# Causal mask products of two self attentions: weights of 32 rows by 128 columns instead of 32 by 32

## What is computed

```python
scores = jnp.einsum('bhqd,bhkd->bhqk', q, k) / math.sqrt(hd)
causal = jnp.tril(jnp.ones((l, l), bool))
scores = jnp.where(causal, scores, -jnp.inf)
att = jax.nn.softmax(scores, axis=-1)
out = jnp.einsum('bhqk,bhkd->bhqd', att, v)
```

## Time and profile before

| | |
|---|---|
| median of 3 runs | 839.37 us (839.31 to 840.55) |
| the profiled execution | 838.6 us |
| its span, first to last instruction | 836.8 us |
| mean granted TensorE clock | 0.998 |
| PE busy | 807.1 us (96%) |
| DVE, ACT, POOL busy | 537.8, 400.9, 261.3 us |
| mask products (line 967) | 1024 matmuls, 19.8 us busy |

### The profile page before, as it was taken

One profiled execution on the slowest core, in us unless ns is written; L12 is line 12 of the kernel. 1 busy time (PEld: TensorE's weight loads), 2 busy tenths in 40 slices (PEclk: granted clock), 3 DMA queues, 4 the chain that ended last, 5 costly groups with the idle time before them and its releaser, 6 DMA issues.

```text
span 836.8 us, 23981 instructions
## 1 busy us (share of the span) xinstructions
PE 807.1 (96%) x10073; PEld 662.7 (79%) x10073; DVE 537.8 (64%) x1379; ACT 400.9 (48%) x989; POOL 261.3 (31%) x311
## 2 busy tenths in 40 slices
PE   8999999999999999999998998999999999999995
PEld 6888887675547787777777787989998899989983
DVE  6675666587886676677776744574466546654666
ACT  4554444558773344455555334463454245424542
POOL 0221422569976632112222368640000100010001
PEclk9999999999999999999999999999999999999999
DMA  9310002222220200000000112330000010000001
GB/s 314 139 53 16 16 22 68 83 52 76 74 63 26 76 20 7 22 22 18 19 18 29 31 40 80 100 102 27 2 3 2 2 52 2 2 1 28 2 2 50
DMA packets 21002, 36.85 MB, mean 44 GB/s; under 512 B 3200, under 2 KB 7424, under 8 KB 20640
## 3 DMA queue, kind: packets, MB, share of 16 engines
q1 hardware_dynamic: 20800, 35.20, 13.6%
q10 hardware_dynamic: 96, 0.13, 0.1%
HBM read 30.86 MB, written 2.10 MB: 39 GB/s over the span
## 4 chain that ended last, share of the span: by engine, by line
PE 81%; DVE 7%; ACT 4%; issue 2%; POOL 2%; DMA 1%; SPq 1%; ACTq 0%; POOLq 0%; DVEq 0%
PE bank L840 16%; PE bank L842 15%; PE bank L841 15%; PE bank L997 6%; PE bank L1277 5%; PE bank L1247 4%; PE bank L1261 3%; PE bank L1017 3%; PE bank L1134 2%; PE bank L1002 2%; DVE tank L2342 1%; PE bank L967 1%; PE bank L1121 1%; PE bank L1298 1%; PE bank L859 1%
## 5 line engine op out<-in xcount | busy, mean ns | idle before, releaser
L840 PE MATMUL bank<-wr,hTl 128*128 128x512 f32 (+3 forms) x392 | 153.3, 391 | 1.3 <-issue 0.8
L842 PE MATMUL bank<-wr,hTh 128*128 128x512 f32 (+3 forms) x392 | 146.9, 375 | 0.0
L841 PE MATMUL bank<-wr,hTh 128*128 128x512 f32 (+3 forms) x392 | 146.5, 374 | 0.0
L1584 ACT ACTIVATE pT<-bank 128x512 f32<-128x512 f32 x128 | 70.0, 604 | 95.1 <-PE bank L967 95.0
L2342 DVE TENSOR_REDUCE tank<-bank 128x4 f32<-128x512 f32 x128 | 82.1, 683 | 42.4 <-PE bank L967 42.4
L840 PEld LDWEIGHTS bank<-wr,hTl 128*128 128x128 f32 (+1 forms) x392 | 73.6, 188 | 17.9 <-issue 5.3
L842 PEld LDWEIGHTS bank<-wr,hTh 128*128 128x128 f32 (+1 forms) x392 | 73.7, 188 | 12.5
L840 PE MATMUL bank<-hTh,wr 128*128 128x256 f32 (+1 forms) x272 | 83.1, 306 | 0.0
L841 PEld LDWEIGHTS bank<-wr,hTh 128*128 128x128 f32 (+1 forms) x392 | 73.8, 188 | 11.2 <-issue 1.0
L841 PE MATMUL bank<-hTl,wr 128*128 128x256 f32 (+1 forms) x272 | 81.0, 298 | 0.0
L842 PE MATMUL bank<-hTh,wr 128*128 128x256 f32 (+1 forms) x272 | 81.0, 298 | 0.0
(11 more groups left out here) (250 smaller groups left out, 1763.8 us busy)
## 6 DMA issues: line engine op xcount, KB each, us to landing
raw<-w_qkv_dram SPq DMA_DIRECT2D x12, 256.0 KB, 2.9
raw<-w_xq_dram SPq DMA_DIRECT2D x16, 192.0 KB, 2.4
raw<-w_xo_dram SPq DMA_DIRECT2D x12, 256.0 KB, 2.8
cin<-xT_dram SPq DMA_DIRECT2D x8, 256.0 KB, 3.9
x_all<-x_dram SPq DMA_DIRECT2D x8, 256.0 KB, 6.6
cin<-ctx_dram SPq DMA_DIRECT2D x8, 256.0 KB, 3.4
cin<-ctxT_dram SPq DMA_DIRECT2D x8, 256.0 KB, 3.3
out_dram<-x_all SPq DMA_DIRECT2D x8, 256.0 KB, 2.1
```

The lines of the kernel that those rows point to most:

```text
L840: mm(dst, lhs[1], rhs[0], start=start, stop=False)
L841: mm(dst, lhs[0], rhs[1], start=False, stop=False)
L842: return mm(dst, lhs[0], rhs[0], start=False, stop=stop)
L1584: av(pT[e][:, 2 * rows + n, :], t_bank[n][:, :], ACT.Exp).then_inc(exp_ready, 1)
```

## The change

The masks' weights are now slices of a banded matrix `band16` (128 partitions by 224 columns, bf16): 96 columns of zeros, the 32 by 32 identity once in each group of partitions, 96 columns of zeros. The slice of 128 columns that begins at column `96 - 32 * g` has the identity in its columns `32 * g` to `32 * g + 31` and zeros elsewhere. A mask product now writes all 128 partitions at the columns of block `g`: what it adds is the triangle in the block's partitions and zero in the others. Its weights have 32 rows and 128 columns, as a score product's, and it takes the same row group as the scores of its bank. The number of mask products stays (16 in a paired step, 8 in an unpaired one) and so do their moving columns (128). They are issued block by block, the straight and the turned ones of one block together; `scores_psum` and `shifted_psum` are incremented after the last block.

The identity blocks come in 32 more columns of the array `masks`; POOL sets the zeros with two memsets in its first microsecond or so, DVE casts 32 columns where it cast 128, and PE waits for these four instead of two. `band16` takes 192 bytes more per partition than `ident16`; what is allocated after it moves by as much.

```diff
-    masks = np.concatenate([np.eye(P), later, sooner], 1)
+    masks = np.concatenate([np.eye(P), later, sooner, np.tile(np.eye(PAD), (GROUPS, 1))], 1)
...
-        ident16, causal16 = sb("ident16", [P, P], BF16), sb("causal16", [P, 2, PAD], BF16)
+        BAND = P - PAD
+        band16, causal16 = sb("band16", [P, BAND + P], BF16), sb("causal16", [P, 2, PAD], BF16)
...
-        causal = view(1, 3840, 2 * PAD)
+        causal = view(1, 3840, 3 * PAD)
...
-        TABLES, EARLY, ROWS = 2, 3, 3
+        TABLES, EARLY, ROWS = 4, 3, 3
...
-            def hide_later(banks, turned_over):
+            def hide_later(banks, turned_over, rows, g, stop):
+
+                at = slice(g * PAD, (g + 1) * PAD)
                 for n in range(2):
-                    for g in range(GROUPS):
-                        rows = (g + 2 * turned_over + n) % GROUPS
-                        at, of = slice(g * PAD, (g + 1) * PAD), slice(rows * PAD, (rows + 1) * PAD)
-                        ins = mm(tiles(banks[n][:, :])[at, :, at], ident16[of, of],
-                                 causal16[of, turned_over, :].unsqueeze(1).broadcast_to([PAD, KT, PAD]), start=False, stop=True,
-                                 skip_group_check=True)
+                    of = slice((2 * rows + n) * PAD, (2 * rows + n + 1) * PAD)
+                    ins = mm(tiles(banks[n][:, :])[:, :, at], band16[of, BAND - g * PAD:BAND - g * PAD + P],
+                             causal16[of, turned_over, :].unsqueeze(1).broadcast_to([PAD, KT, PAD]), start=False, stop=stop,
+                             skip_group_check=True)
                 return ins
...
-                if scored(i):
-                    hide_later(s_bank, 0).then_inc(scores_psum, 1)
-                if scored(j):
-                    hide_later(t_bank, 1).then_inc(shifted_psum, 1)
+                for g in range(GROUPS):
+                    last = g == GROUPS - 1
+                    if scored(i):
+                        ins = hide_later(s_bank, 0, rows, g, True)
+                        if last:
+                            ins.then_inc(scores_psum, 1)
+                    if scored(j):
+                        ins = hide_later(t_bank, 1, rows_c, g, True)
+                        if last:
+                            ins.then_inc(shifted_psum, 1)
...
+            nc.gpsimd.memset(band16[:, 0:BAND], 0.0).then_inc(tables_ready, 1)
+            nc.gpsimd.memset(band16[:, BAND + PAD:], 0.0).then_inc(tables_ready, 1)
...
-                v.tensor_copy(ident16[:, :], ident[:, :]).then_inc(tables_ready, 1)
-                v.tensor_copy(causal16[:, :, :], causal.rearrange("p (a t) -> p a t", a=2)).then_inc(tables_ready, 1)
+                v.tensor_copy(band16[:, BAND:BAND + PAD], causal[:, 2 * PAD:]).then_inc(tables_ready, 1)
+                v.tensor_copy(causal16[:, :, :], causal[:, 0:2 * PAD].rearrange("p (a t) -> p a t", a=2)).then_inc(tables_ready, 1)
```

## The result

The changed kernel is slower: 844.17 us median (843.94 to 844.82, 4 runs) against 839.34 us (838.84 to 840.55, 4 runs), a ratio of 1.0055 with a 95% interval of 1.0042 to 1.0068, so +4.6 us (3.5 to 5.7). The prediction was 841.9 us, in a range of 840.2 to 854.4, with 0.72 on slower. The direction and the range held; the loss is nearly twice the forecast 2.5 us. The question for the experiments is where the other part came from.

A forecast was written before the change was run, and what follows sets the result against it. PE's own stream, busy 96% of the span, was taken as the bound. Entry saved against four rounds gave 54 × 0.027 + 20 × 0.05 = +2.5 us on the median 839.37, so 841.9 us, range 840.2 to 854.4.

The forecast's parts named there:

- PE's stream is the path in both self attentions: Both self attentions: a nanosecond between last score product and first product behind the masks goes into the end nearly whole.
- rival E: Mask places: if DVE or ACT set the steps' length, the time stays; chance held within 0.15 for same.
- 54 paired, 20 unpaired places: Both self attentions: 1024 mask products make 54 paired places of 16 products and 20 unpaired ones of 8.
- Entry saved, exit kept: Around the masks: tile shape change on entering (0.11 us) goes; the one on leaving stays, 0.155 us to the next work.
- Rival C: Entering the masks: fp32 to bf16 stops the array as a new shape does; 8.1 us more, +10.6 us; chance 0.05.
- Pace of a round 0.056 us: Masks' four rounds over four row groups: 128 columns' streaming sets 0.056 us a round, if weight loads keep up.
- A: Mask rounds: weight loads set the pace, 0.112 us a round; in all +14.9 us, 854.3; chance 0.15.
- B: Mask rounds: the load hides only in part, 0.084 us a round; +8.7 us, 848.1; chance 0.07.
- D: Mask rounds: they overlap, so entry is saved and nothing paid; −8 us, 831.4; chance 0.13.
- The sum, +0.027 and +0.05 us a place, +2.5 us: Mask places: 54 paired at +0.027 us and 20 unpaired at +0.05 us, 1.5 + 1.0 = +2.5 us.
- The rest at nothing, ±0.3 us: Outside the mask rounds: later releases of maxima and exponentials, POOL's memsets, DVE's cast, a larger DMA; nothing, ±0.3 us.
- its 0.15 for "same": Whole kernel: chance 0.15 that the time lies within 1.7 us of before; faster 0.13, slower 0.72.

The follow-up runs named there:

- the two kernels with the old pace of the projections: Changed kernel with band16 allocated last, all other tiles at their old places: +0.6 us; changed kernel with 64 bytes more, 256 in all: +1.3 us; both against the kernel before.

## Why the prediction was right or wrong

- *PE's stream is the path in both self attentions.* Right for 76% of added time (13.8 of 18.1 us) and 60 to 67% of removed time (8.4 to 9.3 of 13.9 us), not "nearly whole". The step that was too strong took a few us of waits as negligible; they are small in sum, but they grow and shrink by 4 us with a stream that is 14 to 18 us shorter or longer. For the masks' 1.9 us, +0.6 and +1.3 us were measured in the two kernels with the old pace of the projections, so rival E holds for a part of the places.
- *54 paired, 20 unpaired places.* Right, read from the count.
- *Entry saved, exit kept.* Right: 0.12 us in place of 0.22, and 0.144 us out. Rival C is out. The Trainium skill, "TensorEngine Tiling (Array Packing)", section Tiling Modes, says that a change of mode drains the engine and a change of tile alone does not. The trace agrees: the delay on entering went with the change of mode, and the one on leaving stayed with it.
- *Pace of a round 0.056 us.* Right: by the start times a row group's products come 55 to 56 ns apart, and with it A, B and D fall. The Trainium skill, "TensorE: Matmul & The Clock Gate", section Back-to-back issue gap, gives about 81 ns a product for a stream of pairs of load and matmul with 128 columns. That figure doesn't carry over to rounds over four row groups here: 56 ns a round, with its four loads.
- *The sum, +0.027 and +0.05 us a place, +2.5 us.* Measured are 0.019 and 0.045 us, +1.9 us. The term that was mis-sized is the exit, 0.144 for 0.155, 0.8 us over 74 places; why it is shorter from tiles of 32 by 128 than from 32 by 32 is not shown. (The paired place was also rounded up: 430.875 less 430.85 is 0.025, not 0.027, 0.1 us in the sum.)
- *The rest at nothing, ±0.3 us.* This is the step that failed. It listed waits, memsets, a cast and a DMA, and of the allocation it said nothing, though the description of the change has it: all that is allocated after `band16` moves by 192 bytes. That is +4.9 us in the projections' start sum, +4.7 us (3.5 to 6.0) of time by itself, and nearly all of the result. The forecast's 2.5 us was about half of the loss, for a cause that gives 0.6 to 1.3 us of it.

So that the direction and the range came out right was mostly luck, by another cause than the one named. With the projections at their old pace the change cost 0.6 us (−0.1 to 1.3) in one kernel and 1.3 us (0.6 to 2.1) in the other. Both are under the 1.7 us that the prediction called the least that can be told from no change, and both would have fallen in its 0.15 for "same".

## What to carry to other kernels

A change of a tile's size moves every tile behind it: compare the address of the hot operands before and after, and keep it (put the new tile last, or fill up to the old place modulo 256 bytes, which one kernel here bears out), before the time says anything of the change itself. When a result is off, compare the groups that the change doesn't touch first, as the projections here. Before a difference of a few us is read, compare the granted clock of the runs and of the profiled one: 3.4 us at half clock hid 1.5 us of the gain of the kernel without masks. Trading a change of tile shape (0.1 us) for rounds on fewer tiles pays for up to two further rounds of 128 bf16 columns (0.056 us each), by an estimate from the prices found here: 0.11 us on entering, 0.03 us of starts and 0.01 us on leaving against 0.056 us a round. This change added three.

## What the runs showed that I had not expected

- The pace of a stream of matmuls with weight loads depends on where in SBUF one of the two operands lies: 113 ns against 117 to 120 ns for 256 moving columns, the same instructions, with shifts of 32 to 224 bytes making a difference and 256 bytes none. Over 1992 products it is worth 2.2 to 5.6 us.
- A place that is bad for one shape can be good for another: at a shift of 64 bytes 256 columns are 7 ns slower and 512 columns 3 ns faster.
- A bf16 weight load of 32 rows lasts 93 ns with 128 columns, 134 ns with 127 and 87 ns with 32.
- On a stream that fills 96% of the span, the waits of PE still gave way by 4.3 us when it became 18.1 us longer, and grew by 4.2 us when it became 13.9 us shorter.
